# Attention over normalized image channels on one core: another order of the opening

## The reference

```
def _gn(v, G=32, eps=1e-5):                 # 32 groups of 16 channels
    g = v.reshape(B_, G, C_ // G, H_, W_)
    m = mean(g, (2, 3, 4));  s = var(g, (2, 3, 4))
    return (g - m) / sqrt(s + eps)

xn = _gn(x)
q, k, v = Wq xn, Wk xn, Wv xn               # (b, 8, 64, N) each
attn = softmax(q^T k)                       # over the 2304 keys
out = gamma * (attn v) + Wsc xn
result = x + out
```

## Time and profile before

| | us |
|---|---|
| median of 3 runs | 3167.55 |
| lowest, highest run | 3166.71, 3169.11 |
| profiled execution, its own time | 3167.74 |
| its span, first to last instruction | 3165.9 |
| TensorE busy | 3118.3 (98%) |
| GpSimd busy | 2809.0 (89%) |
| VectorE, ScalarE busy | 2081.5, 2079.9 (66%) |
| mean granted TensorE clock | 0.997 |

### The profile page before, as it was taken

One profiled execution on the slowest core, in us unless ns is written; L12 is line 12 of the kernel. 1 busy time (PEld: TensorE's weight loads), 2 busy tenths in 40 slices (PEclk: granted clock), 3 DMA queues, 4 the chain that ended last, 5 costly groups with the idle time before them and its releaser, 6 DMA issues.

```text
span 3165.9 us, 119190 instructions
## 1 busy us (share of the span) xinstructions
PE 3118.3 (98%) x52592; PEld 2220.2 (70%) x52592; DVE 2081.5 (66%) x3443; ACT 2079.9 (66%) x3377; POOL 2809.0 (89%) x2128
## 2 busy tenths in 40 slices
PE   5999999999999999999999999999999999999998
PEld 3677777777777677776777777777777777767766
DVE  7776666666667666666666766666666666666673
ACT  4666676776666677676666667767666666666675
POOL 2788999999898899999889899999988989889898
PEclk9999999999999999999999999999999999999999
DMA  3010110100011001010001101011000000000000
GB/s 128 26 43 26 30 35 21 35 28 17 26 40 41 25 25 41 15 51 15 19 27 46 40 16 40 25 31 35 21 15 19 17 16 20 16 20 16 20 21 17
DMA packets 92964, 92.08 MB, mean 29 GB/s; under 512 B 44320, under 2 KB 90400, under 8 KB 92448
## 3 DMA queue, kind: packets, MB, share of 16 engines
q1 hardware_dynamic: 92448, 84.44, 8.9%
HBM read 56.10 MB, written 18.87 MB: 24 GB/s over the span
## 4 chain that ended last, share of the span: by engine, by line
PE 91%; POOL 5%; ACT 1%; issue 1%; DVE 0%; POOLq 0%; ACTq 0%; DVEq 0%
PE SL L416 25%; PE PJ L355 18%; PE MX L388 11%; PE OB L437 10%; PE OB L434 9%; PE OB L436 9%; PE PJ L352 6%; POOL PLO L871 4%; PE PJ L372 1%; PE SL L411 1%; ACT PE L526 0%; POOL DF L852 0%; POOL QK L858 0%; ACT L611 0%; DVE mx L673 0%
## 5 line engine op out<-in xcount | busy, mean ns | idle before, releaser
L871 POOL TENSOR_TENSOR PLO<-PE 128x768 f16<-128x768 f32 x1728 | 2496.2, 1467 | 292.4 <-ACT PE L526 292.3
L526 ACT ACTIVATE PE<-SL 128x768 f32<-128x768 f32 x1728 | 1307.3, 810 | 27.4 <-PE SL L416 27.3
L434 PE MATMUL OB<-V,PE 128*128 128x65 f16 x10368 | 1050.5, 193 | 5.6 <-POOL PLO L871 4.7
L436 PE MATMUL OB<-V,PE 128*128 128x64 f16 x10368 | 1050.2, 193 | 0.0
L437 PE MATMUL OB<-V,PLO 128*128 128x65 f16 x10368 | 1049.9, 196 | 0.0
L534 ACT ACTIVATE MXC<-MX 128x384 f32<-128x384 f32 x864 | 423.2, 490 | 939.4 <-PE MX L388 939.4
L670 DVE TENSOR_REDUCE mx<-MX 128x1 f32<-128x384 f32 x864 | 481.3, 557 | 801.2 <-PE MX L388 800.3
L434 PEld LDWEIGHTS OB<-V,PE 128*128 128x128 bf16 x10368 | 964.8, 99 | 56.8 <-POOL PLO L871 13.3
L416 PE MATMUL SL<-QK 64*128 64x384 f16 x10368 | 999.4, 323 | 0.0
L436 PEld LDWEIGHTS OB<-V,PE 128*128 128x128 bf16 x10368 | 962.9, 97 | 36.7
L437 PEld LDWEIGHTS OB<-V,PLO 128*128 128x128 f16 x10368 | 963.8, 98 | 0.0
(11 more groups left out here) (101 smaller groups left out, 1192.2 us busy)
## 6 DMA issues: line engine op xcount, KB each, us to landing
gx<-x SPq DMA_DIRECT2D x36, 768.0 KB, 4.7
xr<-x SPq DMA_DIRECT2D x96, 192.0 KB, 2.4
out<-xr SPq DMA_DIRECT2D x96, 192.0 KB, 1.9
X<-x SPq DMA_DIRECT2D x6, 768.0 KB, 8.6
CR<-c SPq DMA_TRANSPOSE x96, 2.3
QK<-wk SPq DMA_DIRECT2D x1, 1024.0 KB, 12.7
QK<-wq SPq DMA_DIRECT2D x1, 1024.0 KB, 13.4
QK<-wv SPq DMA_DIRECT2D x1, 1024.0 KB, 14.1
```

The costliest lines, as they stand in the source:

```text
L434: pe.matmul(acc, upper, v[:, D:V1], start=k == 0 and h == 0 and i == 0, stop=False, skip_group_check=True)
L436: pe.matmul(acc[:, 0:D], upper, v[:, 0:D], start=False, stop=False, skip_group_check=True)
L526: act.activation(PE32[:, s % PB, :].rearrange("p (h n) -> p h n", h=2), SL[s % 2][:, :, 0:CH], ACT.Exp, scale=1.0 / SS).then_inc(s_exp, 1)
L871: nc.gpsimd.tensor_tensor(PLO[:, s % PB, :], PE32[:, s % PB, :], PE32[:, s % PB, :].bitcast(BF16)[:, 1:4 * CH:2], ALU.subtract).then_inc(s ...
```

## The change

- SyncE loads the weights in the order wk, wv, wq, wsc (`ORDER`), and all engines handle them in this order (`TURN` is a weight's place in it).
- TensorE runs the first small matmul of the norm chain ahead of all transposes, and the second one behind half of those of wk. ScalarE calls Sqrt once on the identity matrix ahead of its first copy, and the Sqrt of the chain behind the first group of wk.
- GpSimd makes no lower half any more; VectorE makes all six. Of the key differences GpSimd makes none before the first top (`s_mx`).
- Pieces 0 and 3 are scaled by ScalarE (`BY_SCALAR`, four Identity instructions with scale and bias), the others by VectorE as before.
- `FIRST` has three v units among the k units: k0 k1 v0 k2 v1 k3 v2 k4 q0 k5. A v unit waits for its own piece alone. `BESIDE` has 8 units for the 11 slots; slots 9 and 10 (counted from 0) have only their tops, slot 8 also the leave of q 5.

The core of the diff:

```diff
-FIRST = tuple(("k", c) for c in range(NCH)) + (("q", 0),)
-BESIDE = (("q", 1), ("v", 0), ("v", 1), ("v", 2), ("v", 3), ("v", 4), ("v", 5), ("q", 2), ("q", 3),
-          ("q", 4), ("q", 5))
+FIRST = (("k", 0), ("k", 1), ("v", 0), ("k", 2), ("v", 1), ("k", 3), ("v", 2), ("k", 4), ("q", 0), ("k", 5))
+BESIDE = (("q", 1), ("v", 3), ("v", 4), ("v", 5), ("q", 2), ("q", 3), ("q", 4), ("q", 5))
+ORDER = (0, 2, 1, 3)
+TURN = {w: i for i, w in enumerate(ORDER)}
+BY_SCALAR = (0, 3)
...
-            for w in range(4):
+            for w in ORDER:
...
-                        pe.wait_ge(s_wf, 4 * (2 if kind == "v" else WEIGHT[kind]) + 4)
-                        if kind == "v":
-                            pe.wait_ge(s_gl[0], NCH // 2)
-                            pe.wait_ge(s_gl[1], NCH // 2)
-                        else:
-                            pe.wait_ge(s_gl[c % 2], c // 2 + 1)
+                        pe.wait_ge(s_wf, CT * TURN[2 if kind == "v" else WEIGHT[kind]] + CT)
+                        pe.wait_ge(s_gl, c + 1)
...
-            weights(0)
             root(0, 0)
+            weights(0, (0, 1))
             root(0, 1)
-            weights(1)
+            weights(0, (2, 3))
+            weights(2)
             for kind, c in FIRST:
-                if kind == "k" and c in (2, 4):
-                    weights(c // 2 + 1)
                 project((kind, 0, c))
+                if (kind, c) == ("v", 0):
+                    weights(1)
+                if (kind, c) == ("k", 4):
+                    weights(3)
...
+            def scale(c):
+                act.wait_ge(s_rstd, 1)
                 for t in range(CT):
+                    one = act.activation(first[:, c, t, :], first[:, c, t, :], ACT.Identity,
+                                         bias=gn_bias[:, t:t + 1], scale=gn_rstd[:, t:t + 1])
+                one.then_inc(s_gt, 1)
...
+            act.wait_ge(s_const, 1)
+            act.activation(MXC[:, 0:P], identf[:, :], ACT.Sqrt)
+            weights(0, (0,))
             act.wait_ge(s_gv, 3)
             act.activation(gn_root, gn_ve, ACT.Sqrt).then_inc(s_gs, 1)
+            weights(0, (1, 2, 3))
+            scale(0)
             upper(0)
-            weights(1)
             upper(1)
+            weights(2)
             upper(2)
             leave(("k", 0, 0))
-            weights(2)
+            scale(3)
             upper(3)
...
-            for i in range(len(BESIDE)):
+            for i in range(LEAD // 2):
                 top_copy(2 * i)
-                if i:
+                if 0 < i <= len(BESIDE):
                     leave((BESIDE[i - 1][0], 0, BESIDE[i - 1][1]))
...
-            for c in range(0, NCH, 2):
-                pool.wait_ge(s_gh, c + 1)
-                nc.gpsimd.tensor_tensor(X[:, 0, 1, :, c * CH:(c + 1) * CH], first[:, c, :, :],
-                                        X[:, 0, 0, :, c * CH:(c + 1) * CH], ALU.subtract).then_inc(s_gl[0], 1)
+            pool.wait_ge(s_mx, 1)
             for c in range(NCH):
                 keys_diff(("k", 0, c))
```

More of the change, by code:

```diff
@@ L209, in build @@
         s_gh = sem("s_gh")
-        s_gl = [sem(f"s_gl{i}") for i in range(2)]
+        s_gl = sem("s_gl")
+        s_gd = sem("s_gd")
         s_gno = sem("s_gno")
@@ L442, in _, with weights @@
             pe.wait_ge(s_const, 3)
-            def weights(w):
+            def weights(w, part=range(CT)):
                 pe.wait_ge(s_wld[w], 16)
-                for t in range(CT):
-                    n = w * CT + t
+                for t in part:
+                    n = TURN[w] * CT + t
                     if n >= 4:
@@ L452, in weights @@
                     last.then_inc(s_w, 1)
-            weights(0)
             root(0, 0)
+            weights(0, (0, 1))
             root(0, 1)
-            weights(1)
+            weights(0, (2, 3))
+            weights(2)
             for kind, c in FIRST:
-                if kind == "k" and c in (2, 4):
-                    weights(c // 2 + 1)
                 project((kind, 0, c))
+                if (kind, c) == ("v", 0):
+                    weights(1)
+                if (kind, c) == ("k", 4):
+                    weights(3)
             pe.wait_ge(s_wf, 16)
             pe.wait_ge(s_const, 8)
-            for i, (kind, c) in enumerate(BESIDE):
+            for i in range(LEAD // 2):
+                u = (BESIDE[i][0], 0, BESIDE[i][1]) if i < len(BESIDE) else None
                 top(2 * i)
-                project((kind, 0, c), 0, 3)
+                if u:
+                    project(u, 0, 3)
                 top(2 * i + 1)
-                project((kind, 0, c), 3, 6)
+                if u:
+                    project(u, 3, 6)
             for n in range(CHUNKS):
@@ L551, in divide, with weights @@
                 one.then_inc(s_wt, 1)
-            def weights(w):
+            def weights(w, part=range(CT)):
+                for t in part:
+                    act.wait_ge(s_w, TURN[w] * CT + t + 1)
+                    act.activation(WT[:, w, 0, t, :], WB[t][:, :], ACT.Copy, scale=WS).then_inc(s_wh, 1)
+            def scale(c):
+                act.wait_ge(s_rstd, 1)
                 for t in range(CT):
-                    act.wait_ge(s_w, w * CT + t + 1)
-                    act.activation(WT[:, w, 0, t, :], WB[t][:, :], ACT.Copy, scale=WS).then_inc(s_wh, 1)
+                    one = act.activation(first[:, c, t, :], first[:, c, t, :], ACT.Identity,
+                                         bias=gn_bias[:, t:t + 1], scale=gn_rstd[:, t:t + 1])
+                one.then_inc(s_gt, 1)
@@ L559, in upper @@
             def upper(c):
-                act.wait_ge(s_gt, c + 1)
+                if c in BY_SCALAR:
+                    act.wait_ge(s_gt, BY_SCALAR.index(c) + 1)
+                else:
+                    act.wait_ge(s_gd, sum(1 for x in range(c) if x not in BY_SCALAR) + 1)
                 act.activation(X[:, 0, 0, :, c * CH:(c + 1) * CH], first[:, c, :, :], ACT.Copy).then_inc(s_gh, 1)
-            weights(0)
+            act.wait_ge(s_const, 1)
+            act.activation(MXC[:, 0:P], identf[:, :], ACT.Sqrt)
@@ L564, in _ @@
+            weights(0, (0,))
             act.wait_ge(s_gv, 3)
             act.activation(gn_root, gn_ve, ACT.Sqrt).then_inc(s_gs, 1)
+            weights(0, (1, 2, 3))
+            scale(0)
             upper(0)
-            weights(1)
             upper(1)
+            weights(2)
             upper(2)
             leave(("k", 0, 0))
-            weights(2)
+            scale(3)
             upper(3)
             leave(("k", 0, 1))
+            leave(("v", 0, 0))
+            weights(1)
             upper(4)
@@ L575, in _ @@
             leave(("k", 0, 2))
+            leave(("v", 0, 1))
+            leave(("k", 0, 3))
+            leave(("v", 0, 2))
             upper(5)
-            leave(("k", 0, 3))
+            leave(("k", 0, 4))
             weights(3)
-            leave(("k", 0, 4))
+            leave(("q", 0, 0))
             leave(("k", 0, 5))
-            leave(("q", 0, 0))
-            for i in range(len(BESIDE)):
+            for i in range(LEAD // 2):
                 top_copy(2 * i)
-                if i:
+                if 0 < i <= len(BESIDE):
@@ L587, in _ @@
                     keys_diff_upper(("k", 0, i))
-            leave((BESIDE[-1][0], 0, BESIDE[-1][1]))
             for n in range(CHUNKS):
@@ L620, in _ @@
                         b, c, t = norm_part(n, m, 4)
-                        act.wait_ge(s_gt, NCH + CT * (NCH * b + c) + t + 1)
+                        act.wait_ge(s_gt, len(BY_SCALAR) + CT * (NCH * b + c) + t + 1)
                         act.activation(X[:, (b + 1) % 2, 0, t, c * CH:(c + 1) * CH], gx[:, t, :],
@@ L732, in weights @@
                 for t in range(CT):
-                    dve.wait_ge(s_wh, w * CT + t + 1)
+                    dve.wait_ge(s_wh, TURN[w] * CT + t + 1)
                     nc.vector.scalar_tensor_tensor(
@@ L742, in scale @@
                         gn_rstd[:, t:t + 1], ALU.subtract, ALU.mult)
-                last.then_inc(s_gt, 1)
+                last.then_inc(s_gd, 1)
             def lower(c):
@@ L747, in lower @@
                 nc.vector.tensor_tensor(X[:, 0, 1, :, c * CH:(c + 1) * CH], first[:, c, :, :],
-                                        X[:, 0, 0, :, c * CH:(c + 1) * CH], ALU.subtract).then_inc(s_gl[1], 1)
+                                        X[:, 0, 0, :, c * CH:(c + 1) * CH], ALU.subtract).then_inc(s_gl, 1)
             nc.vector.memset(gn[:, :, :], 0.0).then_inc(s_gn0, 1)
@@ L773, in _ @@
             dve.wait_ge(s_rstd, 1)
-            scale(0)
             weights(0)
             scale(1)
+            lower(0)
             scale(2)
             lower(1)
+            weights(2)
+            lower(2)
+            scale(4)
+            lower(3)
+            leave(("v", 0, 0))
             weights(1)
[L780 to L783, removed]
+            lower(4)
+            leave(("v", 0, 1))
             scale(5)
+            leave(("v", 0, 2))
```

(7 more changed lines are left out.)

## The result

| | before | with the change |
|---|---|---|
| median, us | 3167.55 (22 runs) | 3162.68 (22 runs) |
| lowest, highest | 3166.71, 3169.75 | 3160.86, 3164.85 |
| profiled execution | 3167.74 | 3162.76 |
| its span | 3165.9 | 3161.0 |
| ratio of the runs, 95% interval | | 0.9983 [0.9976, 0.9989] |

The change saves 4.9 us, 0.15%. The forecast was 3161.0 with a range of 3158.7 to 3163.7: the time is in the range, on the side of "within 0.2%", and 1.7 us above the forecast. The interval leaves out 1, so these runs tell 0.15% from no change; the prediction had taken 0.2% for about the limit.

A forecast was written before the change was run, and what follows sets the result against it. TensorE, 98% busy, was taken as the bound, with time to gain only before the main loop: -7.5 (first top) - 0.85 (slots) + 0.6 + 1.2 (low clock) = -6.55 us, giving 3161.0, range 3158.7 to 3163.7.

The forecast's parts named there:

- within 0.2%: Whole kernel: the outcome that the time differs from the kernel before by no more than 0.2%; chance 0.46.
- The norm chain: Opening: second small matmul at 21.05 instead of 23.48, factors of the norm ready at 23.3, 2.7 us earlier.
- VectorE, ScalarE, the dense stretch: Opening: first projection at 29.5, first v unit at 35.1, then TensorE the limit; first top at 55.6, 7.5 us earlier.
- Rival (b): Opening: the clock falls inside the dense stretch too, or ScalarE scales slower; total 3162.1 to 3164.4; chance 0.20.
- The slots: Eleven slots before the main loop: slots 9 and 10 each 0.42 shorter, -0.85 us; low clock +0.3 in each of two.
- Rival (a): Bare slots before the main loop: the clock does not fall there, -8.4 us, total 3159.2; chance 0.14.
- The clock at the loop's start: First steps of the main loop: half speed after a clock fall in slot 9, +1.2 us, bounds 0 to 2.5.
- the sum's own range: Total if the summed terms hold: 3159.8 to 3162.4, from the clock term's bounds and 0.4 for the walk; chance 0.57.
- The GpSimd term: Opening: 2.2 + 2.8 us of VectorE's slow scaling beside GpSimd go, against 5.0 us for three lower halves it takes over.
- the walk: Opening: instruction-by-instruction timing up to the first top at 55.6; on the kernel before it gives 62.7 for 63.07, good to 0.4.

The follow-up runs named there:

- e1_fill: The change with four extra unused matmuls of 384 columns behind each top of slots 8 to 10: 3159.25 us.
- e4_gpsimd_back: The change with the lower halves of pieces 0, 2 and 4 made by GpSimd again: 3164.99 us.
- e3: The change with the norm chain put back (both small matmuls behind all transposes of wk, Sqrt not called ahead): 3164.78 us.
- e5: The change with pieces 0 and 3 scaled by VectorE again instead of ScalarE: 3165.11 us.
- e2: The change with its v units put back into the slots, the old order of the weights and q 0 behind k 5: 3158.24 us.
- e6: The change with the v units in the slots and the opening ordered for VectorE: 3154.66 us.
- e7: The kernel before with only the change's norm chain edit (small matmuls earlier among wk's transposes, Sqrt called ahead): 3165.52 us.

## Why the prediction was right, and where it was not

**The norm chain.** Right: second L365 at 21.13 (21.05 forecast), VectorE free for work at 23.43 (23.3). The durations were the ones to go by: the transposes at the start ran at 0.87 us for four, though the grant read 1.00.

**VectorE, ScalarE, the dense stretch.** Right. First projection 29.84 (29.5), first v unit 35.41 (35.1), first top 55.91 (55.6), TensorE without a gap from 35.4 to 54.8. The lead was 7.16 where 7.5 was forecast. Rival (b) happened in part and cost nothing: the clock was low from 30.0 to 33.4, and k 0 and k 1 took 5.74 instead of 4.06 (29.84), but the v unit waited for its weight on VectorE anyway, which was whole at 35.3.

**The slots.** Right in sum: 31.04 us for eleven, where 31.26 - 0.85 + 0.6 = 31.0 was forecast, and in both terms: e1_fill, at the high clock, has 30.41 (-0.85), so the low clock cost 0.6. The clock did fall, at the end of slot 8 and not in slot 9. Rival (a) is out, and e1_fill shows what it would have been.

**The clock at the loop's start.** The step that was off is this term, +1.2 us for the first steps of the loop; it measured 3.0. The mechanism was right, the size was not. I took one low stretch of 3.4 us, half of which is lost, less some slack. The trace before had a longer one that I left out. It lies ahead of the one in rows 6: the grants of 0.89 and 0.90 at its ends make it last from about 25.6 to 32.4, 6.8 us, with TensorE at work in it from 28.39 on.

```profile
24.00:26.00 2.00, 0.00 (x0) 0.00 (x0) 1.24 (x9) 0.54 (x2) 0.00 (x0) 0.89 1.05 381
...
32.00:34.00 2.00, 1.48 (x10) 0.91 (x10) 2.00 (x5) 0.77 (x2) 0.41 (x1) 0.90 0.00 0
```

In the change the clock was low for 8 us of the loop (86.95 to 94.9). At half speed the matmuls of the first step take from 86.95 to 90.3, 3.4 us instead of 1.9, so the slack is used up and L699 comes late in turn; TensorE waits for it from there to 91.39, with the clock still low after these 3.4 us of work, and is busy for only 0.94 of the 2 us from 90 to 92. My upper bound of 2.5 was too low as well. That the time still lies in the stated range is luck in part: the sum's own range ended at 3162.4, and the room above it was there for rival (b), which cost nothing. With 3.0 in the sum it would be 3167.55 - 7.16 - 0.22 + 3.0 = 3163.2, the median is 3162.68; part of the difference can be the end of the kernel, of which the prediction has no term.

**The GpSimd term** was only half a term: I counted 2.2 + 2.8 us of stall against 5.0 of new work on VectorE, and let the walk settle it. It came out right for the sum. What it lacked is the other half that e4_gpsimd_back shows: the lower half of piece 0 takes 3.15 us on GpSimd and 1.76 on VectorE, and the first projection waits for it. The walk had this in it, the term did not name it.

**Small slips.** By its own bounds, 0 to 2.5 for the clock and 0.4 for the walk, the sum's range would be 3159.4 to 3162.7 and not 3159.8 to 3162.4. Between the two small matmuls of the norm chain the trace has four instructions of VectorE, not five. Slots 9 and 10 took 2.74 and 2.73, just above the 2.7 that was named. None of them changes the forecast.

**What I did not ask** is whether the v units belong there at all. The prediction had both numbers, 6.0 us of TensorE's time ahead of the slots against 0.85 in them, and still took the part as given. It was the one part of the change that loses.

In sum, at the first top: norm chain about 2.0, lower halves off GpSimd 1.8 (0.3 of it that execution's own later start), ScalarE's scaling 1.1; v units -2.1. They make 2.8 and not 7.16. My reading, not tested, is that each was undone alone in the change, where the others and TensorE's dense stretch hide a part of it. With the v units in the slots the same edits lead by 9.24, and in a better order by 12.37.

## What to carry to other kernels

Work that is moved ahead to shorten a later stretch pays only if the later stretch was limited by it: look at what sets the later pace (here VectorE's 2.84 us a slot) before taking matmuls out of it. And a stretch that TensorE leaves nearly empty is paid for in what comes next, at half speed; a few useless matmuls in it can be cheaper than the idle time. When an elementwise job is split between VectorE and GpSimd, check the durations on VectorE while GpSimd works, and who waits for the slower of the two: here 3.15 us of GpSimd cost VectorE 2.8, and TensorE waited for the 3.15.

## What the runs showed of the hardware

- **With bare slots the spread goes with the clock.** Kernels whose slots are bare spread over 4.0 us (the change, 22 runs), 2.8 (e3 and e4) and 4.2 (e5, 11 runs each); with the slots filled or full it is 0.75 (e1, 6 runs), 0.6 (e2) and 0.6 us (e6, 5 runs each). Fewer runs spread less by themselves, but five or six drawn at random from the change's 22 lie that close in about one case of a thousand, an estimate from these 22 times. The six fastest runs of the change (3160.86 to 3161.56) are the six with a mean grant of 0.998, the other sixteen have 0.997. In the kernels without bare slots the mean does not sort the runs. The kernel before spreads over 3.0 us or a little more, and beside the experiments it has its slowest runs (3169.06 to 3169.81) at 0.998 and 0.999, above the 0.997 of many faster ones; e7 spreads over 1.7. What their spread comes from stays open.
- **The granted clock can read 1.00 while TensorE is slow.** From 19.4 to 23.3 four transposes take 1.05 to 1.09 us, at 37.4 us 0.61, with a grant of 1.00 in both stretches. The transfers beside them do not tell the two speeds apart: in the change four transposes at 24.27 take 0.63 us, in e1_fill four at 24.37 take 1.08, with 379 and 374 GB/s from 24 to 26 and a grant of 1.00 in both.
- **A low clock lasts longer than the bare stretch.** In the change it stayed low for 13.7 us, 8 of them in the loop. In the profiled execution of e5, with the same code in slots and loop, it was low for 6.9 us, 4.1 of them in the loop.
